# Layer norms' rows on ScalarE, the context's normalisation and two low parts on GpSimd, other stage leads

## What is computed

```python
def _layernorm(x): m, v = mean(x), var(x); return (x - m) / sqrt(v + 1e-5)

h = relu(_layernorm(x)); x = x + deg * (h @ Wi.T + b) + a @ (h @ Wj.T)         # layer 0
h = relu(_layernorm(x)); x = x + softmax(leaky(e_src + e_dst), masked) @ (h @ W)  # layer 1
h = relu(_layernorm(x)); x = x + attention(h, 8 heads, masked) @ Wo.T + bo      # layer 2
h = relu(_layernorm(x))                                                         # layer 3
out = elu(head_5(join of elu(head_1..4(h))))                  # five graph attention heads
y = relu(out @ w1 + b1) @ w2 + b2 + out
x = x + layernorm(y) * gamma + beta
```

## Time and profile before

| | |
|---|---|
| median of 3 runs | 1984.97 us (1984.79 to 1987.22) |
| the profiled execution's own time | 1986.96 us |
| its span, first to last instruction | 1985.3 us |
| mean granted TensorE clock | 0.974 of full speed |
| TensorE matmuls, busy | 1872.7 us (94%) |
| VectorE busy | 1727.5 us (87%) |
| ScalarE busy | 1450.5 us (73%) |
| GpSimd busy | 607.5 us (31%) |

### The profile page before, as it was taken

One profiled execution on the slowest core, in us unless ns is written; L12 is line 12 of the kernel. 1 busy time (PEld: TensorE's weight loads), 2 busy tenths in 40 slices (PEclk: granted clock), 3 DMA queues, 4 the chain that ended last, 5 costly groups with the idle time before them and its releaser, 6 DMA issues.

```text
span 1985.3 us, 45990 instructions
## 1 busy us (share of the span) xinstructions
PE 1872.7 (94%) x15944; PEld 1772.0 (89%) x15944; DVE 1727.5 (87%) x6095; ACT 1450.5 (73%) x3378; POOL 607.5 (31%) x756
## 2 busy tenths in 40 slices
...
DMA packets 31206, 43.85 MB, mean 22 GB/s; under 512 B 3328, under 2 KB 26880, under 8 KB 30976
## 3 DMA queue, kind: packets, MB, share of 16 engines
...
...
## 4 chain that ended last, share of the span: by engine, by line
PE 78%; DVE 8%; ACT 5%; issue 5%; POOL 1%; DMA 0%; DVEq 0%; ACTq 0%; POOLq 0%; SPq 0%
PE ps L900 54%; PE ps L929 13%; PE ps L1094 8%; PE ps L1113 3%; DVE lg L1367 2%; ACT pT L861 2%; ACT ea L808 1%; DVE tb L1296 1%; DVE cx L1387 1%; ACT pb L853 1%; ACT ea L799 0%; PE ps L1002 0%; DVE fu L1333 0%; DVE hT L1220 0%; DVE pT L1375 0%
## 5 line engine op out<-in xcount | busy, mean ns | idle before, releaser
L853 ACT ACTIVATE pb<-lg,hmin 128x256 f32<-128x256 f32 x512 | 232.1, 503 | 67.4 <-DVE hmin L1367 67.0
L1094 PE MATMUL ps<-kp,qp 32*128 32x256 f32 x1536 | 251.7, 296 | 3.3 <-DVE hmin L1367 1.7
L708 POOL TENSOR_SCALAR ea<-ea,rs 128x256 f32<-128x256 f32 x256 | 144.2, 575 | 356.7 <-DVE rs L1317 356.6
L735 POOL TENSOR_TENSOR fu<-fu,b_b 128x256 f32<-128x256 f32 x64 | 45.9, 738 | 674.1 <-PE ps L929 674.1
L861 ACT ACTIVATE pT<-ps 128x512 f16<-128x512 f32 x256 | 151.1, 590 | 133.3 <-PE ps L1113 67.4
L1367 DVE CUSTOM_DVE_ANT_0 lg<-ps,maskp 128x256 f32<-128x256 f32 x512 | 195.3, 419 | 55.6 <-PE ps L1094 55.6
L1094 PEld LDWEIGHTS ps<-kp,qp 32*128 32x128 f32 x1536 | 199.3, 186 | 39.4 <-issue 12.3
L900 PE MATMUL ps<-wout,hid 128*128 128x256 f32 x1536 | 219.7, 289 | 3.3 <-ACT hid L867 2.6
L900 PE MATMUL ps<-pT,whs 128*128 128x256 f32 x1536 | 212.6, 288 | 4.8 <-DVE pT L1326 3.0
L900 PE MATMUL ps<-wh,hT 128*128 128x256 f32 x1536 | 205.0, 286 | 0.4 <-DVE cols L1267 0.3
L692 POOL TENSOR_TENSOR rstd<-ve,pow_half 128x2 f32<-128x2 f32 x160 | 118.4, 741 | 280.4 <-DVE ve L1198 280.3
...
## 6 DMA issues: line engine op xcount, KB each, us to landing
...
t_dram<-tb SPq DMA_DIRECT2D x128, 1.0 KB
...
```

The lines of the kernel that those rows point to most:

```text
L708: last = pool.tensor_scalar(ea(g)[:, c, :], ea(g)[:, c, :], rs[g][:, c:c + 1], 1.0, ALU.mult, ALU.mult)
L853: last = act.activation(pb[h % 2][:, c, :], lg[h % 2][:, c, :], ACT.Exp, bias=hmin[h % 2][:, c:c + 1], scale=-1.0)
L1094: last = pe.matmul(bank(BA)[:, c, :], qp[r, a, oc, blk(c)], kp[r, b, oc, :], start=(n == 0), stop=(n == 2))
```

## The change

Five things are done at once. ScalarE writes the rows of norms 0 to 3 with `Identity`, scale `rstd` and bias `nmr`; for that GpSimd makes `nmr` = -mean x rstd, two instructions of one column, behind each power, and waits for its own power first. GpSimd does `normal`, `hid_lo` of head 4 and `f1_lo`. The semaphores follow: `gather` p now waits for GpSimd's `normal` p - 1, and `stats` waits for ScalarE's `rows` of the batch before. The costs in the table of steps are changed with them. And `LEAD` and `GRAIN` have other values. Cut to its core:

```diff
-        GRAIN, LEAD = 0.02, (42.0, 28.0, -2.0, 23.0)
+        GRAIN, LEAD = 0.05, (25.0, 13.0, 11.0, 24.0)
...
-            a("inv_std", n, PO, 0.78, ("var", n))
+            a("inv_std", n, PO, 1.1 if n < 4 else 0.78, ("var", n))
...
-            a("rows", 0, VE, 0.65, ("inv_std", 0), ago("exps", 0), ago("exps", 1))
+            a("rows", 0, SC, 0.8, ("inv_std", 0), ago("exps", 0), ago("exps", 1))
...
-                    a("normal", h // 2, VE, 0.27, ("gather", h // 2))
+                    a("normal", h // 2, PO, 0.5, ("gather", h // 2))
...
-                a("hid_lo", g, *((VE, 0.7) if g == HG else (PO, 1.25)), ("hid_hi", g))
+                a("hid_lo", g, PO, 1.25, ("hid_hi", g))
...
-            a("f1_lo", 0, VE, 0.7, ("f1_hi", 0))
+            a("f1_lo", 0, PO, 1.25, ("f1_hi", 0))
...
-                    pool.tensor_tensor(rstd[n][:], ve[n][:], pow_half[:], ALU.pow).then_inc(rstd_ready[n], 1)
+                    ins = pool.tensor_tensor(rstd[n][:], ve[n][:], pow_half[:], ALU.pow)
+                    if n < 4:
+                        ins.then_inc(rstd_made[n], 1)
+                        pool.wait_ge(rstd_made[n], u + 1)
+                        for c in range(C):
+                            ins = pool.tensor_scalar(nmr[n][:, c:c + 1], mv[n][:, c, 0:1], rstd[n][:, c:c + 1], -1.0,
+                                                     ALU.mult, ALU.mult)
+                    ins.then_inc(rstd_ready[n], 1)
...
+                def low_of_ffn(_, u):
+                    pool.wait_ge(f1_hi, u + 1)
+                    pool.tensor_tensor(f1p[:, 1], rb5[:], f(f1p[:, 0]), ALU.subtract).then_inc(f1_lo, 1)
+
+                def normalise(p, u):
+                    pool.wait_ge(o_used, of(u, p, HQ // 2))
+                    for hh in range(2):
+                        r = rden[:, hh * C:hh * C + C].rearrange("p (c o) -> p c o", o=1)
+                        last = pool.tensor_tensor(two_heads(p)[:, hh], two_heads(p)[:, hh],
+                                                 r.broadcast_to([P, C, DH]), ALU.mult)
...
+                    for c in range(C):
+                        last = act.activation(rows_src(t)[:, c, :], norm_src(n, u)[:, c, :], ACT.Identity,
+                                              bias=nmr[n][:, c:c + 1], scale=rstd[n][:, c:c + 1])
+                    last.then_inc(rows_ready[t], 1)
...
                 def stats_of(n, u):
+                    if n < 4 and u:
+                        dve.wait_ge(rows_ready[row_of(n)], u)
...
-                    after(("ctx",))
+                    if p:
+                        dve.wait_ge(normalised, of(u, p - 1, HQ // 2 - 1))
```

More of the change, by code:

```diff
@@ L126, in adj_preln_kernel @@
         mv = [sb(f"mv{n}", [P, C, 2]) for n in NORMS]
-        ve, rstd = columns_of("ve", 5), columns_of("rstd", 5)
+        ve, rstd, nmr = columns_of("ve", 5), columns_of("rstd", 5), columns_of("nmr", 4)
         ps = ctx.enter_context(nc.psum_tensor("ps", [P, 8 * BANK], F32))
@@ L432, in layers_0_1 @@
             norm_chain(a, 1, ("x1", 0))
-            a("rows", 1, VE, 0.65, ("inv_std", 1))
+            a("rows", 1, SC, 0.8, ("inv_std", 1))
             transposed(a, 1, ("rows", 1), ("x_mi", 0))
@@ L445, in layer_2 @@
             norm_chain(a, 2, ("x2", 0))
-            a("rows", 2, VE, 0.65, ("inv_std", 2), ago("rows_T", 3))
+            a("rows", 2, SC, 0.8, ("inv_std", 2), ago("rows_T", 3))
             transposed(a, 2, ("rows", 2), ago("x3"))
@@ L476, in layer_3 @@
             norm_chain(a, 3, ("x3", 0))
-            a("rows", 3, VE, 0.65, ("inv_std", 3), *(ago("exps", C * HG + c) for c in range(C)))
+            a("rows", 3, SC, 0.8, ("inv_std", 3), *(ago("exps", C * HG + c) for c in range(C)))
             a("x_beta", 0, PO, 1.37, ("rows", 3))
@@ L602, in rows_bank, with two_heads, norm_src @@
             return (BX1, BX1, BA, BB, BX, BY)[t]
+        def two_heads(p):
+            return cx[:, :, 2 * p * DH:(2 * p + 2) * DH].rearrange("p c (h d) -> p h c d", h=2)
         def rows_src(t):
             return (tb1, tb1, cx, cx, tb3[0], fu5)[t]
+        def norm_src(n, u):
+            return xin[u % XI] if n == 0 else fu5 if n == 4 else xs[u % XB]
         def rows_parts(t):
@@ L736, in out_b2 @@
                     last.then_inc(ob_ready, 1)
-                program = dict(inv_std=inverse_std, x_deg=x_deg, scale=scale, v_c=value_third, x_bo=x_bo, x_beta=x_beta, hid_lo=low_of_hidden, out_b2=out_b2)
+                program = dict(inv_std=inverse_std, x_deg=x_deg, scale=scale, v_c=value_third, x_bo=x_bo, x_beta=x_beta, hid_lo=low_of_hidden, out_b2=out_b2, normal=normalise, f1_lo=low_of_ffn)
                 for name, k, u in order:
@@ L1198, in variance @@
                     dve.tensor_scalar(ve[n][:], mv[n][:, :, 1], EPS, None, ALU.add).then_inc(var_ready[n], 1)
-                def norm_rows(n, u):
-                    t = row_of(n)
-                    dve.wait_ge(rstd_ready[n], u + 1)
-                    if u:
-                        if n == 0:
-                            dve.wait_ge(exp_done(0), C * u)
-                        elif n == 2:
-                            dve.wait_ge(rows_T[TR_CTX], u)
-                        elif n == 3:
-                            dve.wait_ge(exp_done(1), head_chunk(HG, C - 1, u - 1))
-                    for c in range(C):
-                        last = dve.tensor_scalar(rows_src(t)[:, c, :], norm_src(n, u)[:, c, :], mv[n][:, c, 0:1],
-                                                 rstd[n][:, c:c + 1], ALU.subtract, ALU.mult)
-                    last.then_inc(rows_ready[t], 1)
                 def low_of_rows(t, u):
@@ L1390, in gather_values @@
                     last.then_inc(o_used, 1)
-                def normalise(p, u):
-                    dve.wait_ge(o_used, of(u, p, HQ // 2))
-                    for hh in range(2):
-                        r = rden[:, hh * C:hh * C + C].rearrange("p (c o) -> p c o", o=1)
-                        last = dve.tensor_tensor(two_heads(p)[:, hh], two_heads(p)[:, hh],
-                                                 r.broadcast_to([P, C, DH]), ALU.mult)
-                    if p == HQ // 2 - 1:
-                        last.then_inc(rows_ready[TR_CTX], 1)
-                    else:
-                        mark(last, ("ctx",))
-                def low_of_ffn(_, u):
-                    dve.wait_ge(f1_hi, u + 1)
-                    dve.tensor_tensor(f1p[:, 1], rb5[:], f(f1p[:, 0]), ALU.subtract).then_inc(f1_lo, 1)
                 def ffn_sum(_, u):
@@ L1427, in result @@
                     last.then_inc(x_final, 1)
-                program = dict(stats=stats_of, aggr=aggregate, var=variance, rows=norm_rows, rows_lo=low_of_rows,
+                program = dict(stats=stats_of, aggr=aggregate, var=variance, rows_lo=low_of_rows,
                                mj_lo=low_of_mj, x_mi=x_plus_own, x1=x_plus_neighbours,
```

37 lines of the change are left out of this document (20 added, 17 removed).

## The result

The changed kernel takes **1975.78 us** (median of 5 runs, 1972.07 to 1978.25), the kernel before 1985.09 us (5 runs, 1984.79 to 1989.73): ratio 0.9944, 95% interval 0.9927 to 0.9961. It is 0.6% faster, by 9 us where 24 were forecast. The profiled execution took 1978.25 us, its span is 1976.6.

The account below looks back on a forecast made before the run. TensorE was taken to bound the middle, with losses left at the ends. Span: 1985.3 - 23.4 - 4 - 5 + 8 + 0.7 = 1961.6 us, median 1961, 1.2% faster; range 1940 to 1986, its own 1950 to 1970.

Parts of the forecast that it names:

- The leads at the end: Last batches: one of two lone passes of 236 matmuls through layer 3 and feed-forward goes, -23.4 us.
- stays as it is: Stretch of layer 2 beside one layer 3, without layers 0 and 1: its 2.8 + 4.6 us over remain unchanged.
- The start: First `hT,wst` comes at matmul 466, not 540, filling part of 7.2 us: -4 us, bounds 0 and 7.2.
- Switches of TensorE: 104 of 2195 rows of TensorE's order go: -5 us, bounds nothing and 10 us.
- Waits in the middle: Tighter covers at `hT` copies, `wp,at` and head 5 add 0.2 to 0.43 us a batch; 0.3 over 27 batches, +8 us.
- the chain of rivals: Rival, chance 0.12: a step comes one GpSimd instruction late (1.3 us) every batch, 35 us more, 1996 us.
- The lone last pass: Remaining pass at the end: longer `hid_lo` 4 and `f1_lo` have less cover, 0 to 1.2 us, taken as +0.7.
- VectorE's load: Instructions of 190.5 us leave VectorE, 5.95 us a batch, so it falls from 92% to 81%.
- It costs and gives nothing where TensorE is the bound: Taking the 190.5 us of instructions off VectorE changes no time in the TensorE-bound middle.
- The sum is the same by both: With or without VectorE and GpSimd blocking each other over SBUF, the forecast time holds, as VectorE has 19% to spare.
- ScalarE's `rows`: Eight more ScalarE instructions a batch at 0.45 us each, 3.6 us a batch, 78% to 84%, hidden.
- GpSimd's guesses: GpSimd's `normal` taken as 0.34 us and `nmr` as 0.2 us an instruction; its load 32% to 44%.

Follow-up runs that it names:

- e1: The kernel before with only the new LEAD and GRAIN, every step on its old engine: 2046.22 us, ratio 1.0306.
- e3: The changed kernel with `rows` of the four norms back on VectorE and no `nmr`: 2038.57 us, ratio 1.0260.
- e4: The changed kernel with `normal`, `hid_lo` of head 4 and `f1_lo` back on VectorE: 1997.22 us, ratio 1.0053.
- e2: The changed kernel with the old LEAD and GRAIN, all moves kept: 2023.25 us, ratio 1.0184.
- e5: The kernel before with 30 more lead for the last layer-3 and feed-forward steps of the last four batches: 1983.34 us, ratio 0.9978.
- e6: The kernel before with 44 more lead for the last layer-3 and feed-forward steps of the last four batches: 1993.48 us, ratio 1.0025.
- e8: The changed kernel, first two batches' `rows` on VectorE without `nmr`, 30 more lead for the last three batches' layer-3 and feed-forward steps: 1997.18 us, ratio 1.0045.
- e10: The changed kernel with three GpSimd adds and `hid_lo` of heads 1 to 3 cut to 16 of 256 columns in batches 4 to 31: 1973.00 us, ratio 0.9937.

## Why the prediction was wrong in size

Forecast for the span were -23.7 us, measured -8.7. The direction and the main mechanism held: one lone pass at the end goes. The 15 us between them are 8.9 at the end, 6.1 at the start and 2.8 in the middle, less 2.2 in the last pass, up to the error of the cuts.

**The leads at the end: the term that failed.** The prediction says that one lone pass goes (-23.4) and that the stretch ahead of it "stays as it is" (2.8 + 4.6 us). The pass went, and e1, e3 and e4 have the same end with the new leads (50 to 54 us), e2 without them has not (71): it is the leads' work. Cut at its own first product the pass held 21.2 us, and the stretch ahead of it 7.9. That stretch did not stay: it holds 14.6 us, because batch 30's own head 5 has no scores of a later batch to hide under, as batch 29's had. So the term is -21.2 + 6.7 = -14.5 us. The trace of before had shown the price, 4.53 us bare. It was moved, not saved, and part of the 7.5 us behind the last scores is TensorE at its lower level. e5, e6 and e8 show how little a count of matmuls behind the last scores says.

**The start: wrong in sign.** Forecast -4, measured +2.1. The gain that was forecast is there, and was eaten. From batch 0's first `q` to batch 1's, and on to batch 2's, before and after:

```profile
79.82:120.85 41.03, 36.14 (x289) 32.24 (x287) 33.54 (x121) 20.59 (x44) 5.33 (x6) 0.92 0.03 8
120.85:170.74 49.89, 47.56 (x367) 44.26 (x367) 40.78 (x145) 32.34 (x78) 10.40 (x15) 0.86 0.05 17
82.24:126.19 43.95, 39.27 (x286) 35.35 (x287) 30.25 (x102) 24.49 (x52) 9.36 (x22) 0.84 0.02 7
126.19:181.40 55.21, 52.85 (x448) 50.17 (x447) 42.52 (x155) 43.29 (x103) 19.98 (x36) 0.97 0.05 16
```

The second stretch went from 7.6 to 3.6 us of stall, with 81 more matmuls in it. But the first rose from 7.7 to 11.0, at a granted clock of 0.84 for 0.92, and batch 0's first `q` itself comes 2.4 us later, with the same work ahead of it. Of these 2.4 us 0.95 is the norm's longer chain, 4.55 us for 3.60. That was in the prediction (4.3), but only as something to be covered; at the start nothing covers it, and e8 gives 1 us back. Some 1.2 us lie ahead of that wait. GpSimd's `normal` is not to blame: TensorE waits 1.64 us for batch 0's context, and in the kernel before it waited longer there, for VectorE:

```profile
115.64 0.66 PE L929 MATMUL ps<-ident,cx 128*128 128x128 f32 x4 [1.93 <-DVE cx L1396]
```

Why the first stretch rose is not attributed.

**Switches of TensorE: -5 is not there.** The middle's stall rose by 5.8 us where waits account for 2.0 (8.6 after 6.6). No run isolates the switches; no gain from having fewer is seen.

**Waits in the middle: +8 forecast.** +2.0 in waits, +5.8 in all. The place was right (`hT` ahead of `wo,hT`), head 5's wait went, and the chain of rivals that would have put GpSimd's queue in TensorE's path did not start: 2.3 us for `cx`. The two terms together gave +3; that the middle came out no further off is luck, since neither came as forecast.

**The lone last pass.** Forecast +0.7, measured -1.5, at a granted clock of 0.84 for 0.78. No run isolates the longer low parts there.

**VectorE's load.** The forecast took 190.5 us of instructions off VectorE; its busy time over the run fell by 66 (1727.5 to 1661.4). The groups that stayed grew by 76 us, the last sum into `xs` alone from 28.6 to 52.5. The remaining 48 us are in the subtraction: groups overlap in the records, before they sum to 2040 us where the engine is busy for 1727.5, so taking a group off frees less than its own busy time. "It costs and gives nothing where TensorE is the bound" failed as a statement on the change: under the new leads, VectorE's work without the moves goes with a loss of 60 us (e1), of which 45 are its instructions held beside GpSimd's. "The sum is the same by both" was nearly right for the changed kernel (e10, 3.5 us in the middle, for the part that it cut) and wrong by 45 us for its leads on their own.

**ScalarE's `rows`.** 544 ns against 452 by busy time over count: 8 instructions x 0.092 = 0.7 us a batch more, hidden. GpSimd's guesses held, 293 for 340 and 267 for 200 ns, and its 44% in the middle too.
